# A gated cross-attention and quantised feed-forward block on one core: first row of maxima ahead of loads, a maximum over partitions on TensorE, third buffers in the last stage, and another order in the last group

## The reference

```python
def _layernorm(x, axis=-1, eps=1e-05):
    m = jnp.mean(x, axis=axis, keepdims=True)
    v = jnp.var(x, axis=axis, keepdims=True)
    return (x - m) / jnp.sqrt(v + eps)
...
# attention: B=32, S=256, D=512, 16 heads of 32
scores = jnp.einsum('bhqd,bhkd->bhqk', q, k) / jnp.sqrt(jnp.asarray(dk, q.dtype))
p = jax.nn.softmax(scores, axis=-1)
x = jnp.einsum('bhqk,bhkd->bhqd', p, v)
...
def _act_fake_quant(x, clip_factor):
    scale = jax.nn.sigmoid(clip_factor) * jnp.max(jnp.abs(x)) / QMAX
    return jnp.clip(_ste_round(x / scale), -QMAX - 1.0, QMAX) * scale
...
xq = _act_fake_quant(x, clip_x[0])          # I = 1408
gate = jnp.einsum('bsh,ih->bsi', xq, _weight_fake_quant(w_gate))
up = jnp.einsum('bsh,ih->bsi', xq, _weight_fake_quant(w_up))
h = _act_fake_quant(jax.nn.silu(gate) * up, clip_down[0])
return jnp.einsum('bsi,hi->bsh', h, _weight_fake_quant(w_down))
...
x = x + jnp.tanh(g_xattn[0]) * attention(_layernorm(x), ctx_1024)
x = x + jnp.tanh(g_ffn[0]) * ffn(_layernorm(x))
```

## Time and profile before

| | before |
|---|---|
| median of 3 runs | 1734.7 us (1734.4 to 1735.49) |
| the profiled execution | 1731.45 us |
| its span in the trace | 1729.3 us |
| busy, share of the span | PE 93%, DVE 75%, ACT 49%, POOL 32% |
| attention stage | 0 to about 1202 us |
| gate and up | about 1214 to 1541 us |
| down | about 1544 to 1729 us |

### The profile page before, as it was taken

How to read it: one execution, slowest core, us unless ns; L and a number is a source line. 1 busy time by engine, 2 the same in 40 slices (tenths; PEclk the granted TensorE clock), 3 DMA queues, 4 the chain that set the end, 5 groups by cost and what they waited for, 6 DMA issues and landing times.

```text
span 1729.3 us, 31276 instructions
## 1 busy us (share of the span) xinstructions
PE 1601.9 (93%) x11748; PEld 752.0 (43%) x11748; DVE 1302.7 (75%) x2085; ACT 840.5 (49%) x1122; POOL 558.9 (32%) x782
## 2 busy tenths in 40 slices
PE   4879999999999999999999999985999999989888
PEld 2334544444445444444454444433444444434333
DVE  5638788787887887878878778676687778778766
ACT  4443534535336344353353533524677777757440
POOL 5423514335234242351432523212000000008778
PEclk9989999999999999999999999999899999999999
DMA  8668769788687687886968777635344552027996
GB/s 243 167 173 180 176 160 206 166 199 171 179 182 185 171 191 179 193 176 170 204 160 203 174 180 141 168 71 198 116 183 182 207 200 98 25 82 296 424 413 229
DMA packets 301108, 320.75 MB, mean 185 GB/s; under 512 B 176432, under 2 KB 225584, under 8 KB 298032
## 3 DMA queue, kind: packets, MB, share of 16 engines
q1 hardware_dynamic: 299248, 318.72, 67.8%
q10 hardware_dynamic: 1728, 0.27, 0.1%
HBM read 180.49 MB, written 100.27 MB: 162 GB/s over the span
## 4 chain that ended last, share of the span: by engine, by line
PE 44%; issue 25%; DVE 11%; DMA 7%; ACT 6%; POOL 4%; SPq 3%; POOLq 0%; ACTq 0%; DVEq 0%
PE bank L1492 10%; PE bank L1380 10%; PE bank L1382 9%; PE bank L1381 9%; PE spair L1469 5%; DMA x<-out_dram 4%; DVE mx L1032 4%; POOL yh L712 3%; ACT pr L755 2%; PE spair L1444 2%; DMA stacks<-mT 2%; SPq L412 1%; ACT wf L825 1%; DVE wi L1120 1%; DVE bst L982 1%
## 5 line engine op out<-in xcount | busy, mean ns | idle before, releaser
L1032 DVE TENSOR_REDUCE mx<-spair 128x4 f32<-128x1024 f32 x256 | 301.1, 1217 | 33.9 <-PE spair L1444 33.4
L755 ACT ACTIVATE pr<-spair 128x1024 f32<-128x1024 f32 x256 | 258.0, 1019 | 125.4 <-PE spair L1469 125.4
L1009 DVE SCALAR_TENSOR_TENSOR parts<-bank,bqk,parts 128x512 f16<-128x512 f32 x128 | 96.0, 750 | 177.8 <-ACT parts L744 176.4
L1600 PE MATMUL spair<-xqT,wgT 128*128 128x512 bf16 x704 | 182.5, 382 | 1.0 <-ACT xqT L910 1.0
L1600 PE MATMUL spair<-xqT,wuT 128*128 128x512 bf16 x704 | 182.1, 381 | 0.0
L1469 PE MATMUL spair<-stacks 128*128 128x256 f16 x1024 | 154.2, 277 | 24.8 <-DMA stacks<-mT 14.4
L744 ACT ACTIVATE parts<-bank,bqk 128x512 f16<-128x512 f32 x128 | 87.7, 685 | 153.4 <-PE bank L1382 153.4
L868 ACT ACTIVATE sil<-spair,gsc 128x512 f32<-128x512 f32 x176 | 118.3, 680 | 78.8 <-PE spair L1600 78.7
L618 POOL TENSOR_TENSOR cl<-cbuf,ch 128x512 f16<-128x512 f32 x64 | 79.0, 1235 | 236.4 <-ACT ch L732 236.4
L712 POOL TENSOR_TENSOR yh<-yh,x 128x512 f32<-128x512 f32 x64 | 134.7, 2136 | 48.7 <-DVE yh L1328 25.0
L1492 PE MATMUL bank<-pr,v 128*32 128x256 f32 x2048 | 137.9, 387 | 12.3 <-ACT pr L755 7.6
(11 more groups left out here) (187 smaller groups left out, 3324.4 us busy)
## 6 DMA issues: line engine op xcount, KB each, us to landing
stacks<-qk_spill SPq DMA_DIRECT2D x384, 128.0 KB, 4.0
qk_spill<-parts SPq DMA_DIRECT2D x64, 512.0 KB, 5.1
x<-out_dram SPq DMA_DIRECT2D x32, 1024.0 KB, 11.1
h_spill<-hb SPq DMA_DIRECT2D x10, 2816.0 KB, 9.2
xbuf<-in_x_dram SPq DMA_DIRECT2D x16, 1024.0 KB, 7.2
cbuf<-in_ctx_dram SPq DMA_DIRECT2D x16, 1024.0 KB, 6.7
xres<-in_x_dram SPq DMA_DIRECT2D x16, 1024.0 KB, 5.6
out_dram<-xres SPq DMA_DIRECT2D x16, 1024.0 KB, 4.6
```

Of the source, the lines that this page charges most:

```text
L755: act.activation(pr[:, u % 4, :, :, :].rearrange("p a b q -> p (a b q)"), spair[u % 2][:, :, :].rearrange("p a q -> p (a q)"), ACT.Exp, sc ...
L1009: dve.scalar_tensor_tensor(out=parts[:, c, 2 * w + 1, :], in0=pj[(g + 1) % 3][:, :], scalar=bqk[:, w, c:c + 1], in1=parts[:, c, 2 * w, :], ...
L1032: dve.tensor_reduce(mx[:, h:h + 2, b, :], spair[u % 2][:, :, :].rearrange("p a (q k) -> p a q k", q=KH), AX_X, ALU.max).then_inc(max_done, 1)
L1600: last = pe.matmul(spair[k % 2][:, s, :], w[:, t, kc * P:kc * P + P], xqT[:, par, kc, :], start=(kc == 0), stop=(kc == KC - 1))
```

## The change

- **Start of ACT's queue.** `high_x(0, t)` stands ahead of `w_high(0)` and `constants()`.
- **First body.** On SP the row of maxima `mrow(0)` stands ahead of `stack(0, None, 2)`, `stack(0, None, 3)` and the loads of x and ctx of group 2 and of the residual; ctx is loaded ahead of x. On PE `turn_max(0)` stands ahead of `qk(1, 0)`.
- **Group 14's x1** (in the body with i = 15) is made on DVE after the last `key_max`, but for its first tile.
- **Group 15.** Tile 0 is projected by PE after score 15 where it was after score 13, tile 1 only after the last `pv`; DVE does its first `x1_tile` after the last `norm`, and the ends of tile 2 move behind `x1_measure`.
- **Maximum over partitions.** DVE multiplies the identity by M1, PE multiplies a matrix of ones with it into `pj[2]`, DVE reduces along the row. POOL runs its reduction once on a constant (`warm`). The copy of `csb` moves behind `first_ints`.
- **Down.** `xq`, `xqT` and `sil` are now parts of one tensor, `ffn_work`; its two halves serve in the last stage as third buffers of x1 and y. SP loads x1 for m + 3, and `y_tile(m)` waits for the store of y(m - 3). The load of x1 for m = 2 is issued during the last gate-and-up group. POOL's loop is unrolled.

```diff
+            for t in range(NT):
+                high_x(0, t)
             w_high(0)
             constants()
-            for t in range(NT):
-                high_x(0, t)
...
             stack(0, None, 1)
-            stack(0, None, 2)
-            stack(0, None, 3)
-            load_x(2)
-            load_c(2)
             wait(sp, stack_ready, 2)
-            wait(sp, w_hi, 1)
-            wait(sp, w_lo, 1)
-            load_res(0)
...
                 mrow(j)
-                if not first:
+                if first:
+                    stack(0, None, 2)
+                    stack(0, None, 3)
+                    load_c(2)
+                    load_x(2)
+                    wait(sp, w_hi, 1)
+                    wait(sp, w_lo, 1)
+                    load_res(0)
+                else:
...
             def body(i, j, par, before):
+                if j == 0:
+                    turn_max(0)
                 if i is not None:
                     qk(i, 0, par, before)
-                turn_max(j)
+                if j > 0:
+                    turn_max(j)
...
-                    if i is None and g >= NGR - 3:
-                        oproj(j, g - (NGR - 3), None)
+                    if i is None and g == NGR - 2:
+                        oproj(j, 0, None)
...
-                for t in range(NT) if i is not None else range(2, NT):
+                for t in range(NT) if i is not None else range(1, NT):
                     oproj(j, t, i)
...
-                        if g == 6:
-                            x1_tile(j, 0)
-                            x1_tile_stats(j, 0)
-                            x1_tile_ends(0)
...
-                    for t in range(1, NT):
+                    for t in range(NT):
                         x1_tile(j, t)
                         x1_tile_stats(j, t)
-                        if t < NT - 1:
+                        if t < 2:
                             x1_tile_ends(t)
                     x1_measure(j)
-                    x1_tile_ends(NT - 1)
+                    for t in range(2, NT):
+                        x1_tile_ends(t)
                     x1_far_ends()
...
-            pool.wait_ge(m1_part, 1)
-            pool.partition_all_reduce(small[:, M1A:M1A + 1], small[:, M1:M1 + 1], P, RMAX).then_inc(m1_all, 1)
+            pool.partition_all_reduce(small[:, SPARE2:SPARE2 + 1], small[:, S1:S1 + 1], P, RMAX).then_inc(warm, 1)
+            pool.wait_ge(warm, 1)
...
+            dve.wait_ge(m1_part, 1)
+            dve.wait_ge(diag_mm, 1)
+            dve.tensor_scalar(diag[:, 0, :], id32[:, :], small[:, M1:M1 + 1], None, ALU.mult).then_inc(m1_part, 1)
             x1_shifts(NG - 1)
-            dve.wait_ge(diag_mm, 1)
-            dve.tensor_copy(csb[:, :], obank[:, :]).then_inc(colsc_ready, 1)
+            dve.wait_ge(m1_spread, 1)
+            dve.tensor_reduce(small[:, M1A:M1A + 1], pj[2][:, 0:P], AX_X, ALU.max).then_inc(m1_all, 1)
...
+            pe.matmul(pj[2][:, 0:P], ones32[:, :], diag[:, 0, :], start=True, stop=True).then_inc(m1_spread, 1)
...
+        y3 = [y_two[:, 0, :, :], y_two[:, 1, :, :], work_two[:, 1, :, :]]
+        r3 = [x2[:, 0, :, :], x2[:, 1, :, :], work_two[:, 0, :, :]]
...
+            wait(sp, f_turned, NG * 2)
+            wait(sp, gu_mm, (NG - 1) * 2 * IC)
+            load_res3(2)
+            load_h(0)
             for m in range(NG):
...
-                if m + 2 < NG:
-                    load_res3(group_of[m + 2], m % 2)
+                if m + 3 < NG:
+                    load_res3(m + 3)
                 if m + 1 < NS:
                     load_h(m + 1)
```

## The result

| | before | changed |
|---|---|---|
| median | 1735.1 us (1734.4 to 1736.56, 4 runs) | 1704.05 us (1703.26 to 1706.35, 4 runs) |
| profiled execution, its span | 1731.45, 1729.3 us | 1703.26, 1701.3 us |
| SP issues the last row of maxima | 1151.49 us | 1140.58 us |
| first matmul of gate and up | 1213.64 us | 1197.47 us |
| PE's first and last group of the down stage start | 1546.95, 1712.61 us | 1530.62, 1687.08 us |

The ratio is 0.9822, interval 0.9811 to 0.9834. The predicted time was 1703.0. So some 3 us of the agreement between 31.7 predicted and 31.05 measured stands in no row of the two traces, and one term of 3.0 in the prediction did not come. So the closeness of the two is in part luck: by the traces the change gives 28.0.

The account below looks back on a forecast made before the run. PE, the busy engine, was held back by waits, and transfers set the down stage's pace. Terms 3.0 + 11.4 + 0 + 1.9 + 3.9 + 11.5 = 31.7 us, so 1734.7 - 31.7 = 1703.0 us; eight in ten 1698 to 1709.5.

Parts of the forecast that it names:

- Start: Start of the kernel: ACT's new order lets x's transposes be issued earlier; 3.0 us, between 0 and 3.3.
- run of eight transposes: Start, SP's queue: issuing x's eight transposes takes 12.9 us, from 14.1 to 27.0; only its end counts.
- first rival: Start and down stage: transposes wait behind weight loads (start 0 to 1), POOL ends at 1718 (down 8); 1708 us, chance 0.20.
- The second half of the argument: Start: ctx's transposes follow x's on the same queue, so PE's wait for turned ctx moves from 46.52 to about 43.3.
- Row of maxima: First body: PE's whole 10.6 us wait for the first row goes, plus 0.8 from the clock; 11.4 us (10.6 to 12).
- Group 14: Last attention body: making group 14's x1 after the maxima gains 0, with up to 0.2 lost where PE doesn't wait.
- Group 15: Last attention group: one projection, not two, ahead of the last pv; gain 1.9 us, between 0.5 and 2.6.
- Maximum over partitions: Between last x1 and scale SX: the way by PE takes 2.1 us, not 6.0; gain 3.9 us, 3.3 to 4.4.
- Down stage: Last stage: third buffers save one 9.5 us step and 2 at the end; 11.5 us, bounds 8 to 13.
- Is POOL fast enough?: End of down stage: POOL's 16 adds from 1686 end by 1714 to 1718, PE's last tile 1713; at 1718 gain 8.
- POOL is locked out: Rival, down stage: DVE's passes exclude POOL's adds, 10.6 us a group, stage gains 0; 1714.5 us, chance 0.04.
- nine batches of 16 us: Rival, down stage: third buffer slows transfers from 11.9 us a batch; at 16 us, 1738 us; chance 0.02.

Follow-up runs that it names:

- ACT's order alone: Kernel before with only ScalarE's first operations reordered, high part of x ahead of that of the first weight: 1734.49 us, ratio 1.0004.
- Wo late: Changed kernel with the load of Wo issued behind the transposes of x, its conversion behind those of x and ctx: 1706.61 us, ratio 0.9837.
- h moved: Changed kernel with loads of spilled h on SP one group earlier (1708.75 us), one later (1703.97 us) or two later (1715.59 us).

## Why the prediction was right, and where it was not

**Start, 3.0 predicted, nothing measured.** The step of the prediction that failed is the run of eight transposes, carried over from the earlier trace rows as "issue of 12.9 us from 14.1, so 27.0". It is no fixed length: it ran from 14.42 to 30.74, 16.3 us, because the first two issues took 7.8 us and not 3.75. The DMA engines were full from 12 to 22 us (share 1.05, 391 GB/s) with the weights that stood ahead, and SP could not hand over the next transfer. The prediction named the queue as its first rival and weighed it from the wrong side: it asked when transposes land, not how long SP is held in issuing them. ACT's order alone gave 1.0004, and Wo moved away gave the issue time back. The second half of the argument, that the turned ctx follows with SP and releases PE near 43.3, stays open. It came at 46.52, as before, since SP was not ahead; and in the one run in which SP was 3 us ahead, Wo stood ahead of ctx in the queue.

**Row of maxima, 11.4 predicted.** At the third group of scores PE is 11.4 us earlier (104.69 to 93.30), 10.6 of it the wait and 0.8 the clock. The second row of maxima is issued 10.9 us earlier and so is the last (1151.49 to 1140.58), those between 10.1 to 10.9. The other half microsecond was gone by the second body. The part alone gave 11.1. Right.

**Group 14, 0 predicted.** No term shows: from PE's turn of the last maxima to the first `pv` of the last body it takes 5.95 us in before and 5.93 now. This part was not run alone.

**Group 15, 1.9 predicted, 1.3 measured.** The first `pv` of the last body is 10.93 earlier than in the earlier trace rows's kernel and the last one 12.24 (1185.73 to 1173.49). Between the first and second `pv` 0.5 was lost: PE's granted clock was 0.72 from 1147 to 1149 in the changed kernel, and back at 1.00 in the corresponding stretch of before, 1158 to 1160. The order itself gave 1.8, as worked out; the hole of 3.05 became 0.35. Only the two traces show this; it was not run alone.

**Maximum over partitions, 3.9 predicted.** 3.96 in the traces, 3.8 with the change undone there (4.9 by medians). The 2.1 us were 2.08. The warm-up was costed at nothing for a reason that fell: the second reduction does not need it.

**Down stage, 11.5 predicted, 11.7 measured.** 165.7 less 156.5 is 9.2, and the tail is 16.7 less 14.2, so 2.5. (The prediction took 2 there and read 4.3 us from DVE's last tile to the end of the last add; by the earlier trace rows it is 1726.80 less 1723.00, so 3.8, and now 1.3.) On buffers and transfers the reasoning held at each step: the pace stayed at 11.9 and the last waiting tile became y(12), so PE had three groups left and not four. With two buffers the stage is 165.9 again. "Is POOL fast enough?" came out well: 64 adds took 133.8 us, 8.4 a group, and the last add follows the last tile.

The prediction's reading of these adds was wrong, though. It said that an add beside DVE's passes is slowed to 2.0 us but goes on. 2.0 is a mean of two kinds. Of the changed kernel's 64 adds 39 take 1.3 us, 27 of them beside the scaling of a tile (L1349), and 25 take 2.6 to 4.1, each of them beside one of the two passes of `h_quant` (L1342 and L1344). DVE and POOL in the changed kernel, the passes first without adds, then with them (each add in a window of its own, since the view puts adds in a row together):

```profile
1538.62 3.09 DVE L1342 TENSOR_SCALAR wuT<-yh 128x5632 bf16<-128x5632 f32 x1 [2.62 <-ACT yh L939]
1541.75 1.63 DVE L1344 TENSOR_SCALAR wuT<-wuT 128x5632 bf16<-128x5632 bf16 x1
...
1633.92 3.08 DVE L1342 TENSOR_SCALAR wuT<-hk 128x5632 bf16<-128x5632 f32 x1
1634.17 3.95 POOL L725 TENSOR_TENSOR yh<-yh,x 128x512 f32<-128x512 f32 x1 [2.79 <-DMA x<-out_dram]
1637.04 2.58 DVE L1344 TENSOR_SCALAR wuT<-wuT 128x5632 bf16<-128x5632 bf16 x1
1638.09 2.64 POOL L725 TENSOR_TENSOR yh<-yh,x 128x512 f32<-128x512 f32 x1
1640.69 1.26 POOL L725 TENSOR_TENSOR yh<-yh,x 128x512 f32<-128x512 f32 x1
```

The first add ends 1.12 us after the first pass, the second pass 1.50 after that add, the second add 1.11 after the second pass: they take turns. The second pass lasts 2.58 beside adds, in all 14 groups that have them, and 1.63 without. So for these two passes the exclusion of the Trainium skill (SBUF — State Buffer, SBUF: two separate sides), a lock held for the whole instruction, agrees with the trace. (The page ties it to a two-port mode of VectorE's; the trace does not name the mode of a pass.) What was wrong is the price of the rival "POOL is locked out": its 5.7 us of passes hold the wait for an add already. Without it they are 4.7, which with 4.9 of adds makes 9.6 a group (an estimate) beside PE's 9.5, and not 10.6. POOL was locked out by these passes, and it cost the stage next to nothing.

**Sum.** 0 + 10.9 + 1.3 + 4.0 + 11.7 = 27.9, the 28.0 between the spans. (In the prediction's rivals one sum does not come out: nine batches of 16 us instead of 11.9 add 36.9 to 1703.0, which is 1739.9 and not 1738.) The other 3 us of the medians' 31.05 stay open. Executions do scatter by as much: in the nine traces of kernels that have the changed kernel's attention code word for word (its own, and all variants of it but that with Wo late), SP issues the last row of maxima between 1140.2 and 1146.0. The two that stand at 1140.2 and 1140.6 are those in which PE's wait for the turned ctx was short (1.2 and 1.5 us; the others waited 3.3 to 3.7). With ACT's old order all three traces have a short wait (0.9 to 1.9), with the new one two of ten (these nine, and ACT's order alone). So the new order goes with a longer wait behind the queries, and mostly with a lower clock behind that; its time alone, 1.0004, shows no loss by it. The profiled executions of before and changed are both of the kind with the full clock.

## What to carry to other kernels

When a queue is full, the issuing engine is held as well: a transfer that is ready earlier is issued into the same queue and gains only what stands ahead of it, so look at what the queue holds and not at when the operand is there. If transfers set the pace of a stage, an extra buffer is worth one step of the slower engine and not the sum of its waits; then ask, for each transfer in the queue, whose deadline is nearest, since a load moved forward delays every store behind it and one moved too far back becomes the bound itself. And an earlier start of the busy engine is no gain when its next operand doesn't move: the longer wait ahead of that can cost it its clock. Lastly, a mean duration can hide two kinds of instruction: an add of 2.0 us on average was one of 1.3 us, or one that had stood still behind a pass.

## What the runs showed of the hardware

- The issue of one DMA transpose took 5.24 us with 5 MB of loads issued ahead in SP's queue (changed kernel), 1.98 with one load of 1 MB less (Wo late), and 1.26 later on.
- POOL's reduction over partitions starts 5.6 to 5.7 us after the MODIFY_POOL_CONFIG ahead of it when its operand is there, and at once after a wait of 337 us, also when it is the first in the program.
- POOL's f32 adds (1.3 us) and DVE's two passes from f32 to bf16 and bf16 to bf16 took turns: 25 adds of 64 took 2.6 to 4.1 us, and the second pass 2.58 and not 1.63. Beside DVE's scaling out of a bank the adds kept their 1.3.
- A second queue did not relieve the first: with h on ACT's queue the two had 53.3% and 48.3% of the engines, and a store took 22.3 us (one 27.8) where it had taken 17.4.
- Reads and writes together held 416 to 421 GB/s on one core over stretches of 75 to 90 us, in before, in the changed kernel and with h moved.
- Of nine traces in which PE had waited 3.3 us or more ahead of the first keys, eight had a granted clock of 0.57 to 0.79 from 44 to 52 us; of five with 0.9 to 1.9 us none had. With the same order of the first body, the first maxima were turned 1.9 to 3.2 us later for it.
